# Feed-forward's two middle layers: both parts of the values in one 512-column pass per weight chunk, the halves added on evacuation

## The reference

```
def _L1_ffn_ref(x, w1_w, w1_s, w2_w, w2_s, h1_w, h1_s, h2_w, h2_s, w3_w, w3_s):
    D_IN, D_HID = (512, 2048)
    def _tlin(x, w, s):
        return jnp.einsum('bsi,oi->bso', x, w) * s
    h = jax.nn.silu(_tlin(x, w1_w, w1_s)) * _tlin(x, w2_w, w2_s)
    h = jax.nn.gelu(_tlin(h, h1_w, h1_s), approximate=False)
    h = jax.nn.gelu(_tlin(h, h2_w, h2_s), approximate=False)
    return _tlin(h, w3_w, w3_s)
...
    x = x + _L1_ffn_ref(_layernorm(x, axis=-1), L1_ffn_w1_w, ...)
```

## Time and profile before

| | us |
|---|---|
| median of three runs (lowest, highest) | 1406.88 (1405.14, 1409.73) |
| profiled execution | 1404.22 |
| its span | 1402.4 |
| PE busy | 1329.9 |
| DVE busy | 904.0 |
| ACT busy | 679.1 |
| matmuls of the two middle layers (L2128), busy | 184.5 |
| output layer's matmuls (L2141), busy | 21.9 |

### The profile page before, as it was taken

How to read it: one execution, slowest core, us unless ns; L and a number is a source line. 1 busy time by engine, 2 the same in 40 slices (tenths; PEclk the granted TensorE clock), 3 DMA queues, 4 the chain that set the end, 5 groups by cost and what they waited for, 6 DMA issues and landing times.

```text
span 1402.4 us, 23487 instructions
## 1 busy us (share of the span) xinstructions
PE 1329.9 (95%) x9866; PEld 1136.3 (81%) x9866; DVE 904.0 (64%) x1131; ACT 679.1 (48%) x754; POOL 12.0 (1%) x18
## 2 busy tenths in 40 slices
PE   7999999999999999896899999999898889999998
PEld 6899999889999986665577777777655669999997
DVE  4665666766566656697778888888425667444443
ACT  4534444544444442652377777777303144555442
POOL 0000000000000000000000000000100000000000
PEclk9999999999999999895899999999999999999999
DMA  8111011401010030120089899999920315455552
GB/s 284 35 31 35 20 42 50 124 20 35 20 35 20 20 121 21 71 80 13 30 318 343 344 341 336 341 344 357 348 90 0 120 64 189 172 183 188 186 185 79
DMA packets 50219, 197.66 MB, mean 141 GB/s; under 512 B 12112, under 2 KB 20560, under 8 KB 30416
## 3 DMA queue, kind: packets, MB, share of 16 engines
q1 hardware_dynamic: 47792, 187.41, 36.8%
q0 software_dynamic: 2336, 8.91, 1.8%
HBM read 195.78 MB, written 0.52 MB: 140 GB/s over the span
## 4 chain that ended last, share of the span: by engine, by line
PE 85%; DVE 10%; issue 2%; ACT 1%; DMA 1%; SPq 0%; POOL 0%; POOLq 0%; DVEq 0%; ACTq 0%
PE psum L453 13%; PE psum L2128 13%; PE psum L428 13%; PE psum L1538 8%; PE psum L480 5%; PE psum L1558 4%; PE psum L1541 4%; PE psum L505 4%; PE psum L2110 3%; PE psum L1561 2%; PE psum L2141 2%; PE psum L1570 1%; PE psum L1958 1%; PE psum L464 1%; PE psum L1827 1%
## 5 line engine op out<-in xcount | busy, mean ns | idle before, releaser
L1599 DVE TENSOR_TENSOR arena_r<-ring,arena_r 128x2048 fp32r<-128x2048 f32 x96 | 219.7, 2290 | 35.7 <-ACT arena_r L1593 35.4
L453 PE MATMUL psum<-ring_r,arena_r 128*128 128x256 f32 x1536 | 201.4, 290 | 3.5 <-ACT arena_r L723 2.5
L453 PEld LDWEIGHTS psum<-ring_r,arena_r 128*128 128x128 f32 x1536 | 192.1, 194 | 4.2 <-issue 2.7
L428 PE MATMUL psum<-arena_r 128*128 128x512 f32 x768 | 186.0, 398 | 9.3 <-ACT arena_r L757 9.2
L1593 ACT CAST arena_r<-ring 128x2048 fp32r<-128x2048 f32 x96 | 183.5, 1913 | 16.5 <-PE psum L1541 10.8
L2128 PE MATMUL psum<-arena_r 128*128 128x256 f32 x1536 | 184.5, 283 | 1.1 <-DVE arena_r L2187 1.1
L2128 PEld LDWEIGHTS psum<-arena_r 128*128 128x128 f32 x1536 | 184.4, 192 | 1.2 <-issue 1.2
L428 PEld LDWEIGHTS psum<-arena_r 128*128 128x128 f32 x768 | 143.1, 190 | 41.6 <-issue 8.4
L2081 DVE TENSOR_TENSOR arena_r<-ring,arena_r 128x2048 fp32r<-128x2048 f32 x44 | 100.9, 2292 | 117.0 <-ACT arena_r L2076 117.0
L2076 ACT CAST arena_r<-ring 128x2048 fp32r<-128x2048 f32 x44 | 83.8, 1904 | 111.4 <-PE psum L2128 85.2
L1538 PE MATMUL psum<-arena_r 128*128 128x512 f32 x512 | 132.5, 401 | 1.3 <-issue 1.3
(11 more groups left out here) (309 smaller groups left out, 1692.5 us busy)
## 6 DMA issues: line engine op xcount, KB each, us to landing
ring<-in_stream SPq DMA_DIRECT2D x151, 1024.0 KB, 4.9
arena<-in_ctxT POOLq DMA_DIRECT2D x8, 1024.0 KB, 12.3
arena<-in_ctxT SPq DMA_DIRECT2D x7, 1024.0 KB, 7.9
arena<-in_wk SPq DMA_DIRECT2D x16, 256.0 KB, 3.3
wv_in<-in_wv SPq DMA_DIRECT2D x8, 512.0 KB, 3.4
arena<-in_wq SPq DMA_DIRECT2D x16, 256.0 KB, 2.5
arena<-in_wk SPq DMA_DIRECT2D x16, 128.0 KB, 3.2
arena<-in_wo SPq DMA_DIRECT2D x2, 1024.0 KB, 6.3
```

The lines of the kernel that those rows point to most:

```text
L428: last = nc.tensor.matmul(bank, wk_sb[wp][:, c, w], cx[xp][kb][:, c, :], start=c == wp == xp == 0, stop=c == C - 1 and xp == 1)
L453: last = nc.tensor.matmul(bank[:, q * T:(q + 1) * T], cx[xp][kc // 4][:, c, kc % 4 * P:(kc % 4 + 1) * P], wv_sb[wp][:, c, :], start=c == w ...
L1599: nc.vector.tensor_tensor(mwlo[p % MB], ring[(BLK_MOE + p) % RING][:, :], mwhi[p % MB].bitcast(fp32), ALU.subtract).then_inc(moe_lo if p < ...
```

## The change

The two value parts move into one tensor (`heven` and `hodd` of shape 2 x 16 x 256), so that one matmul can stream both behind one weight chunk: 512 columns, high part's products in columns 0 to 255 of the PSUM bank, low part's in 256 to 511. The weights' low part still goes over the values' high part alone, 256 columns, added to the lower half. On evacuation the upper half is copied by ACT to a new tensor `fsum`, DVE adds the lower half from PSUM, and Gelu reads the sum from SBUF. `ffn_act` and `ffn_lo` now count two steps per block, and the numbers in the waits follow.

```diff
-        heven = [view(o + i * FC * T, FC, T, one_pass=True) for i in range(2)]
+        heven = view(o, 2, FC, T, one_pass=True)
...
+        fsum = view(o, 4, T)
+        o += 4 * T
...
@@ ffn_pe: middle layers
-                        pe.wait_ge(ffn_act, it * RING + (FC * (layer + 1) + s - 3))
+                        pe.wait_ge(ffn_lo, it * (2 * RING) + (2 * (layer * FC + s) + FC - 2 * RING + 1))
                         for c in range(FC):
                             if c == 0:
-                                pe.wait_ge(ffn_lo, FC * (layer + 1) - 1)
+                                pe.wait_ge(ffn_lo, FC - 1 if layer == 0 else 3 * FC - 2)
                             if c == FC - 1:
-                                pe.wait_ge(ffn_lo, FC * (layer + 1))
-                            for wp, xp in PARTS:
-                                last = nc.tensor.matmul(psum[:, 4 + s, 0:T], w[wp][:, c, :], src[xp][:, c, :],
-                                                        start=c == wp == xp == 0, stop=c == FC - 1 and wp == 1)
+                                pe.wait_ge(ffn_lo, FC if layer == 0 else 3 * FC)
+                            nc.tensor.matmul(psum[:, 4 + s, :], w[0][:, c, :], src[:, :, c, :], start=c == 0, stop=False)
+                            last = nc.tensor.matmul(psum[:, 4 + s, 0:T], w[1][:, c, :], src[:, 0, c, :],
+                                                    start=False, stop=c == FC - 1)
...
@@ ffn_scalar: middle layers
                         split_hi(act, j0 + s + 2, it)
-                        act.wait_ge(ffn_lo, it * RING + (done + s - 3))
                         act.wait_ge(blk_used, it * RING + (BLK_W12 + j0 + s + 1))
-                        nc.scalar.activation(fhid[:, s:s + 1, :], psum[:, 4 + s, 0:T].unsqueeze(1), ACT.Gelu,
+                        nc.scalar.copy(fsum[:, s:s + 1, :], psum[:, 4 + s, T:].unsqueeze(1)).then_inc(ffn_act, 1)
+                        act.wait_ge(ffn_lo, it * (2 * RING) + (done + 1))
+                        nc.scalar.activation(fhid[:, s:s + 1, :], fsum[:, s:s + 1, :], ACT.Gelu,
                                              scale=col[:, ds(it * RING + (COLS[name][0] + s), 1)]).then_inc(ffn_act, 1)
-                        act.wait_ge(ffn_act, it * RING + (done + s + 1))
-                        nc.scalar.copy(dst[0][:, ds(it * RING + s, 1), :], fhid[:, s:s + 1, :]).then_inc(ffn_hi, 1)
+                        act.wait_ge(ffn_act, it * (2 * RING) + (done + 2))
+                        nc.scalar.copy(dst[:, 0, ds(it * RING + s, 1), :], fhid[:, s:s + 1, :]).then_inc(ffn_hi, 1)
...
@@ ffn_dve: middle layers
                         split_lo(dve, j0 + s + 2, it)
+                        dve.wait_ge(ffn_act, it * (2 * RING) + (FC + 2 * (layer * FC + s) + 1))
+                        nc.vector.tensor_tensor(fsum[:, s:s + 1, :], fsum[:, s:s + 1, :], psum[:, 4 + s, 0:T].unsqueeze(1),
+                                                ALU.add).then_inc(ffn_lo, 1)
                         dve.wait_ge(ffn_hi, it * RING + (layer * FC + s + 1))
```

More of the change, by code:

```diff
@@ L2042, in build @@
         o = 0
-        heven = [view(o + i * FC * T, FC, T, one_pass=True) for i in range(2)]
+        heven = view(o, 2, FC, T, one_pass=True)
         o += 2 * FC * T
-        hodd = [view(o + i * FC * T, FC, T, one_pass=True) for i in range(2)]
+        hodd = view(o, 2, FC, T, one_pass=True)
         o += 2 * FC * T
@@ L2137, in ffn_pe @@
                 if n in (0, FC - 1):
-                    pe.wait_ge(ffn_lo, 3 * FC - (n == 0))
+                    pe.wait_ge(ffn_lo, 5 * FC - 2 * (n == 0))
                 for b in range(B):
                     for wp, xp in PARTS:
-                        last = nc.tensor.matmul(psum[:, b, :], heven[xp][:, n, b * P:(b + 1) * P], w[wp][:, n % 4, :],
+                        last = nc.tensor.matmul(psum[:, b, :], heven[:, xp, n, b * P:(b + 1) * P], w[wp][:, n % 4, :],
                                                 start=n == wp == xp == 0, stop=n == FC - 1 and wp == 1)
@@ L2158, in ffn_scalar @@
             for layer, (dst, name) in enumerate(((hodd, "h1_s"), (heven, "h2_s"))):
-                j0, done = FC // 2 + layer * FC, FC * (layer + 1)
+                j0 = FC // 2 + layer * FC
                 with act.Fori(0, FC // RING) as it:
                     for s in range(RING):
+                        done = FC + 2 * (layer * FC + s)
                         split_hi(act, j0 + s + 2, it)
-                        act.wait_ge(ffn_lo, it * RING + (done + s - 3))
                         act.wait_ge(blk_used, it * RING + (BLK_W12 + j0 + s + 1))
-                        nc.scalar.activation(fhid[:, s:s + 1, :], psum[:, 4 + s, 0:T].unsqueeze(1), ACT.Gelu,
+                        nc.scalar.copy(fsum[:, s:s + 1, :], psum[:, 4 + s, T:].unsqueeze(1)).then_inc(ffn_act, 1)
+                        act.wait_ge(ffn_lo, it * (2 * RING) + (done + 1))
+                        nc.scalar.activation(fhid[:, s:s + 1, :], fsum[:, s:s + 1, :], ACT.Gelu,
                                              scale=col[:, ds(it * RING + (COLS[name][0] + s), 1)]).then_inc(ffn_act, 1)
-                        act.wait_ge(ffn_act, it * RING + (done + s + 1))
-                        nc.scalar.copy(dst[0][:, ds(it * RING + s, 1), :], fhid[:, s:s + 1, :]).then_inc(ffn_hi, 1)
+                        act.wait_ge(ffn_act, it * (2 * RING) + (done + 2))
+                        nc.scalar.copy(dst[:, 0, ds(it * RING + s, 1), :], fhid[:, s:s + 1, :]).then_inc(ffn_hi, 1)
             for j in (NFFN - 2, NFFN - 1):
@@ L2185, in ffn_dve @@
                                                          ALU.mult, ALU.mult))
[L2186 to L2187 removed]
+                link(dve, nc.vector.tensor_copy(heven[:, 0, n, :], fhid[:, f, :]))
+                nc.vector.tensor_tensor(heven[:, 1, n, :], fhid[:, f, :], heven[:, 0, n, :].bitcast(fp32),
                                         ALU.subtract).then_inc(ffn_lo, 1)
```

4 lines of the change are left out of this document (2 added, 2 removed).

## The result

The changed kernel is slower: median 1414.59 us over 18 runs (1409.05 to 1423.95) against 1405.08 us over 18 runs of the kernel before, ratio 1.0062 with a 95% interval of 1.0046 to 1.0079. The forecast was 9.5 us and 1416.4, with the range 1410.5 to 1421.

A forecast was written before the change was run, and what follows sets the result against it. PE bounds the kernel before; after the change a ring of ScalarE and VectorE, 5.69 us a block, does. First layer +8.20, between layers +1.32, second layer -1.05, output layer +1.04: +9.5 us on 1406.88, forecast 1416.4, range 1410.5 to 1421.

The forecast's parts named there:

- ring without loads: Length of the ring per block in the middle layers without table loads: 5.69 us, bounds 5.52 and 5.84.
- first to 16th cast: First middle layer: 15 turns of 5.69 us plus 9.43 for table loads, 94.78 us instead of 86.40.
- between the layers: From the 16th cast to the next, PE waits for the last values: 7.08 us instead of 5.76, +1.32.
- second layer: Middle layer without table loads: 15 turns of 5.69 us, 85.35 against 86.40, -1.05.
- start of the output layer: Output layer starts 0.84 us behind the last cast, where before it started 0.20 ahead: +1.04.
- The ring: Middle layers: cast, VectorE's weight low part, add, Gelu, high copy, next cast follow each other and set the pace.
- The table loads: First layer, seven loads in the ring: 1.30 us each ahead of Gelu, 1.41 ahead of the cast, 9.43 together.
- Rival A: Loads ahead of Gelu stay hidden under VectorE's work: 4 x 1.30 us fall away, +4.3, 1411.2; chance 9%.
- Rival C: Table loads cost more in the ring than their rows show: 9.0 us more, 1425.4; chance 3%.
- PE's pace: Middle layers' matmuls: a chunk from 360 to 348.7 ns, a block from 5.76 to 5.58 us, 5.8 at most.
- Rival B: Idle time swallows the evacuation, PE runs at 5.58 us a block: 5.8 less, 1401.1; chance 7%.
- Rival D: Clock falls in PE's gaps of 1.4 us; four blocks at half clock cost 22 us; chance 3% beyond slack.

The follow-up runs named there:

- The changed kernel with the parts side by side: Changed kernel with both parts of each piece of values adjacent in SBUF; middle layers 192.57 us against the changed kernel's 192.66, whole-kernel ratio 1.0101 to the kernel before.
- the evacuation's part alone: Changed kernel with PE's old three passes of 256 columns per chunk; middle layers 194.04 us against 184.38 before, whole-kernel ratio 1.0074.
- five variants with the add first: Changed kernel, add ahead of weights' low part: alone 181.21 us, passes grouped by width 179.78, parts adjacent 177.93, tiny early Gelu 179.64, adjacent and grouped 179.72.
- add first with the parts side by side: Changed kernel with VectorE's add ahead of the weights' low part and both value parts adjacent in SBUF; middle layers 177.93 us, ratio 0.9958 to the kernel before.
- the control: Kernel before with one tiny Gelu ahead of the middle layers' loops, so no table loads in them; middle layers 184.38 us as before, ratio 0.9979.

## Why the prediction was right

By the steps of its sum, on the profiled executions:

| step | predicted | measured |
|---|---|---|
| ring without loads | 5.69 (5.52 to 5.84) | 5.65 |
| first cast earlier | -0.18 | -0.10 |
| first to 16th cast | +8.38 | +7.46 (93.86 us) |
| between the layers | +1.32 | +1.27 (7.03 us) |
| second layer | -1.05 | -1.47 (84.93 us) |
| start of the output layer | +1.04 | +1.12 |
| sum | +9.5 | +8.3 |

**The ring.** The mechanism is shown, not only argued: swapping two steps on VectorE takes 11.5 us, lengthening the ring by 0.33 adds that in every block. Of its terms the add was shorter (0.41, not the 0.48 of an instruction with a column operand), the hop 0.13 instead of 0.15, Gelu to the high copy 0.64 instead of 0.60, since Gelu from SBUF took 0.51. Together they come to 0.04 less; each turn of the loop adds 0.08. (The long bound of the ring adds up to 5.83, not 5.84.)

**The table loads.** Forecast 1.30 and 1.41 us, measured 1.27 (6.91 - 5.64) and 1.39, of which 0.08 is the turn of the loop. Seven of them are then 9.0 and not 9.43, and taking them out shortened the way from the first to the 16th cast by 9.0 (93.86 to 84.88), 1.28 each. Rival A falls with the rows: the load ahead of Gelu starts at 1202.43, 0.11 after the add's end (1201.91 + 0.41). Rival C falls with them too: the next instruction starts 0.01 us behind each load.
The Trainium skill's drain of 1.38 us per switch ("ScalarE: Activation LUTs", "What ACT_TABLE_LOAD costs") does not show, neither in the ring (1.28 us for each load taken out) nor outside it (0.02 from the load's end to Gelu).

**PE's pace, the term that was mis-sized.** I took 228.6 + 120.1 = 348.7 ns a chunk, 5.58 us a block, from two rows in which one width followed itself. The changed kernel took 353.5 in most blocks. PE's own gain was therefore 3.4 us, not 5.8. It hardly touched the forecast, because the ring was the longer of the two; but it makes the two almost level in layer 2 (5.655 and 5.64), where PE is busy without a hole and the gaps of 0.11 us that I expected are missing. It also spoils a sign: PE's busy time in the middle layers was to fall by 5.8 us and fell by 1.1. The windows of the changed kernel, one in each layer:

```profile
1200.00:1280.00 80.00, 74.29 (x415) 63.06 (x414) 38.92 (x38) 45.67 (x56) 0.00 (x0) 1.00 0.49 174
1300.00:1360.00 60.00, 60.00 (x342) 52.05 (x341) 33.12 (x32) 31.04 (x43) 0.00 (x0) 1.00 0.53 191
```

So my sentence that the ring alone decides is right for layer 1 (PE idle 5.7 of 80 us) and cannot be told from a tie by this trace in layer 2. The changed kernel with the parts side by side settles it: PE took 5.55 to 5.62 us for ten of the 16 blocks of its layer 2, and the casts still needed 84.82 us from the 17th to the 32nd, against 84.93. So the ring decides there too, and PE's pace added 0.1 us. At 5.76 a block, in the evacuation's part alone, PE decides (86.41). Rival B would have brought 3.4 at best. Rival D does not occur here: the clock is 1.00 in both windows, and over the whole stretch. It is no empty fear, though: with 0.33 us more in the ring it did occur, at the change of layers, for 0.7 us. The remaining difference of 1.2 us is mostly the ring's 0.04 to 0.05 in 30 blocks.

**What was luck.** That the two medians differ by just the 9.5 us of the forecast. The mechanism was worth 8.3; the profiled execution had 1.3 more from code ahead of the middle layers that is the same in both kernels, and the base of three runs, 1406.88, was 1.8 above the median of 18.

**What was not foreseen** is that the loss was so cheap to avoid: with the add ahead of the weights' low part the changed kernel is ahead of the kernel before. The profiled stretches are 3.2 to 6.5 us shorter in all five variants with the add first, and in four of them the whole kernel's interval lies below 1 as well; the best, add first with the parts side by side, had 0.9958 (0.9937 to 0.9978). The whole kernel's times alone would not carry this: the control, with nothing gained in its stretch, had 0.9979.

## What to carry to other kernels

An engine's idle time hides a new instruction only if nobody who sets the pace waits for what stands behind it. Before counting matmuls saved, write down the ring that a new cross-engine wait closes, with every long instruction ahead of the awaited one in its engine's order, and compare it with the pace that is left; then put the short awaited instruction ahead of the long one. Look for table loads behind the new wait: in a loop entered with another function's table they return in every turn, and one tiny call of the function ahead of the loop removes them.

## What the runs showed of the hardware

- The same alternation of a 512- and a 256-column matmul ran at 353.5 or at 346.5 ns a pair, at clock 1.00, mostly for whole blocks, with a change only after PE had waited, and for no cause that the runs found. It is worth 3 us here and hides or feigns small effects of other edits, as it did in the run with the parts side by side.
- A table load between two dependent instructions cost 1.27 to 1.31 us, its own 1.28 and little else, and the loop's eight loads cost nothing where ScalarE waited for PE anyway.
- Two VectorE adds without a wait between them start 0.33 us apart, though each is shown with 0.41.
- A loop turn costs ScalarE 0.08 us where nothing hides it: high copy to the next cast 0.40 instead of 0.32, seen only in the ring.
- After 2.41 us in which PE was idle its granted clock was 0.50, and pairs of matmuls took 0.64 us instead of 0.35; behind idle times of 1.35 to 1.57 us in the same kernel it stayed at 1.00.
